# Layer 0's experts store rows in slot order by the sync queue, and GpSimd gathers each token's rows by slot in the middle phase

## The chip, the cores and the metric

The kernel runs on one core of a Trainium2 chip. The metric is the device time of one execution in microseconds (us). Names of engines: PE is TensorE, DVE is VectorE, ACT is ScalarE, POOL is GpSimd, SP is the sync engine, which computes nothing and issues DMAs. A DMA issued by GpSimd with a list of row numbers is called an indirect DMA here: a gather reads rows from DRAM by number, a scatter writes them by number.

## What is computed

Two transformer layers on x of shape 16 x 256 x 128 (4096 tokens of 128 numbers, f32). Each layer is an attention and a mixture of eight experts, both behind a layer norm, a modulation and a gate. For the change, this is what matters of layer 0's experts and what follows:

```python
logits = xt @ gate_w                                  # 4096 x 8
top_logits, top_idx = jax.lax.top_k(logits, 2)        # two experts for each token
router_probs = jax.nn.softmax(masked, axis=-1)        # over the two
exp_mask = exp_mask * (exp_rank < cap)                # a place beyond the capacity counts for nothing
h = gelu(einsum('ecd,edh->ech', exp_batches, c_fc) + fc_bias)      # d 128, h 512
exp_out = einsum('ech,ehd->ecd', h, c_proj) + proj_bias
out = einsum('nec,ecd->nd', cb_weight, exp_out)       # two weighted rows for each token
...
x = x + gb * out
h = layernorm(x) * (1 + ca) + sa                      # layer 1 starts: q, k, v and an importance
importance = (relu(h @ wi1.T + bi1) @ wi2.T + bi2)    # top 30% of keys by importance are kept
```

## The kernel before, in words

x stays in SBUF as 32 blocks (NT) of 128 tokens. Work on all tokens goes in NCH = 8 chunks of four blocks.

**Route phase.** Every (token, choice) pair is given a slot. Slots are ordered by expert in halves of 128; there are SC = 71 halves, in XTILES = 40 tiles: 31 pair tiles with two halves and 9 single tiles with one. DVE computes for each pair its slot (`slot_i`), and through one-hot matmuls the inverse: for each slot the token that it holds (`r.token`) and the row of `y_dram` to which its result goes (`r.dest`). `y_dram` has a row for each (choice, token) pair in token order, and further rows for the results of empty slots.

**Expert phase** (`expert_phase`, used by both layers; `gated` is true for layer 1 alone). For tile j GpSimd gathers the tokens' rows of `h_dram` (L2186), eight tiles ahead (ROWS). PE transposes them (L2023), ACT copies the transposed rows (L2083). PE multiplies with the first weights into `ps_h` (L2014), ACT applies gelu (L2075), PE multiplies with the second weights into `ps_o` (L2033), DVE adds the bias into `y` (L2121, `finish`). There are four buffers of `y` (UNROLL), and `y_free` waits until the store of the tile four before has landed. GpSimd scatters `y` into `y_dram` (L2196), one indirect DMA for each half. The weights of all experts lie in SBUF; since the expert of a tile is known only on the chip, ACT copies those of a tile into one of four working sets (`copy_weights`, L2052 to L2054), a tile ahead of use. SP loads weights of the next phase (`ahead`) and the `gates`, waits until all stores have landed, and issues `choice_rows` for the first two chunks (LEAD): for each chunk and choice one plain load of 256 KB from `y_dram` into `got`. The block ends with a barrier of all engines.

**Middle phase** (`middle_phase`). SP issues `choice_rows` for chunks 2 to 7. For each chunk ACT scales the first choice's rows (`weigh`, L1164), DVE adds the scaled second choice's rows (L1249), GpSimd multiplies with the gate (`gate`, L1083), DVE adds to x (L1231) and takes mean and variance, ACT and DVE form `std`, `rstd` and `shift` (L1257), ACT normalizes (L1176), PE transposes, ACT modulates, PE and ACT form queries, keys, values and the importance, and DVE counts for each key how many are more important (`rank`, L1276). The engines' orders are written by hand over steps i = 0 to 10; ACT's step i begins with `weigh(i + 1)`, DVE's has `statistics(i - 1)`, `weigh(i)`, `invert(i - 1)`, `rank(i - 3)` and `keys_values(i - 2)`. Between the first two gates GpSimd fills three constant tables: `before`, `head_mask` and `places` (L1086 to L1097). Layer 1's sparse attention comes next.

Layer 1's experts run `expert_phase` with `gated` and end in a final phase with the same kinds of loads. They keep their order.

Of the kernel before, what the change touches and what calls it, by code (L numbers as in the profile page):

```python
# [18 lines left out]
P = 128  # L19
# [996 lines left out]

def middle_phase(nc, k, r, a):
# [6 lines left out]
    with ExitStack() as ctx:  # L1024
# [9 lines left out]
        before = sb("before", [P, 2, T])  # L1034
# [22 lines left out]
        back, h_ready, const_ready = sem("back_m"), sem("h_ready_m"), sem("const_ready_m")  # L1057
        w_turned, w_copied, wi2_ready, pool_step = sem("w_turned1"), sem("w_copied1"), sem("wi2_ready"), sem("pool_step_m")
# [10 lines left out]
        @block.sync  # L1069
        def _(sp):  # L1070
            for n in range(LEAD, NCH):
                choice_rows(sp, k, r, n)

        @block.gpsimd
        def _(pool):
            step = Chain(pool, pool_step)

            def gate(n):
                pool.wait_ge(both_ready, 4 * (n + 1))
                if n == 0:  # L1080
                    pool.wait_ge(gates_in, 16)
                y = view(both[:, n % 2, 0, :], 0, [[2 * C, 2], [C, 2], [1, C]])
                pool.tensor_tensor(y, y, view(gates[:, 2 * n, :], 0, [[C, 2], [0, 2], [1, C]]), ALU.mult).then_inc(gated, 1)  # L1083

            gate(0)
            step(pool.memset(before[:, :, :], -TINY))  # L1086
            step(pool.affine_select(out=before[:, :, :], in_=before[:, :, :], compare_op=ALU.is_gt, fill=0.0, base=0,
                                    pattern=[[P, 2], [-1, T]], channel_multiplier=1))

            step(pool.memset(a.head_mask[:, :], 1.0))  # L1090
            for p in range(4):
                m = a.head_mask[4 * HD * p:4 * HD * (p + 1), :]
                step(pool.affine_select(out=m, in_=m, compare_op=ALU.is_ge, fill=0.0, base=0,
                                        pattern=[[-HD, 4]], channel_multiplier=1))
                step(pool.affine_select(out=m, in_=m, compare_op=ALU.is_ge, fill=0.0, base=HD - 1,
                                        pattern=[[HD, 4]], channel_multiplier=-1))
            pool.iota(a.places[:, :], [[1, KEPT]], base=0, channel_multiplier=0,  # L1097
                      allow_small_or_imprecise_dtypes=True).then_inc(const_ready, 1)
            for n in range(1, NCH):
                gate(n)  # L1100
# [126 lines left out]
        def _(dve):  # L1227
            def statistics(n):
                dve.wait_ge(gated, n + 1)
                xs = k.x[:, 4 * n:4 * n + 4, :]  # L1230
# [20 lines left out]

            def invert(n):
# [13 lines left out]
            def rank(n):  # L1266
                dve.wait_ge(col_turned, n + 1)
                if n == 0:
                    dve.wait_ge(const_ready, 1)
# [13 lines left out]
            for i in range(STEPS):  # L1283
# [417 lines left out]
def route_phase(nc, k, r, name, biased, capacity, weights):  # L1701
# [7 lines left out]
    with ExitStack() as ctx:  # L1709
# [27 lines left out]
        slot_i, part_i = sb("slot_i", [P, KT], I32), sb("part_i", [P, 2, KT], I32)  # L1737
# [59 lines left out]
        def _(dve):  # L1797
# [100 lines left out]
            step(dve.tensor_scalar(r.token[:, :], token_f[:, :], 0.0, None, ALU.max))  # L1898
            step(dve.scalar_tensor_tensor(out=free[:, :], in0=owner[:, :], scalar=0.0, in1=slot_id[:, :],
# [11 lines left out]

def choice_rows(sp, k, r, n):
# [7 lines left out]
def expert_phase(nc, k, r, name, weights, gated, ahead):  # L1920
# [10 lines left out]
    with ExitStack() as ctx:  # L1931
# [41 lines left out]

        def moved(j, ring=UNROLL):
# [4 lines left out]
        def _(sp):  # L1979
# [66 lines left out]
        def _(act):  # L2046
# [10 lines left out]
            if resident:  # L2057
                act.wait_ge(r.weights_in, 16 * E * (nf + 1))
                act.wait_ge(tables_in, 16 * (nf * FK + nr))
                if gated:  # L2060
                    act.wait_ge(halved, 1)
                copy_weights(0)
                copy_weights(1)
            for n in range(-1, XTILES + 1):
# [15 lines left out]
                if exists(n):  # L2080
# [3 lines left out]
                    if resident and exists(n + 1) and n >= 1:  # L2084
# [3 lines left out]
        def _(dve):  # L2088
# [22 lines left out]
            def y_free(j):  # L2111

                wait(dve, stored[j % UNROLL], 16 * moved(j - UNROLL))
                dve.nop(nofuse=True)

            def finish(j):
# [5 lines left out]
                                  each(out_b, j), ALU.add).then_inc(y_ready, 1)  # L2122

# [35 lines left out]
            held = {}  # L2159
            for j in range(-1, XTILES + 1):  # L2160
# [11 lines left out]
                elif exists(j):  # L2172
                    finish(j)

        @block.gpsimd
        def _(pool):
# [24 lines left out]
            for j in range(XTILES + 1):  # L2201
                if not gated and exists(j - 1):
                    scatter(j - 1)
# [3 lines left out]
                if exists(j + ROWS):  # L2207
# [3 lines left out]
                    elif j == 0:  # L2211
# [3 lines left out]
                if gated and exists(j - 1):  # L2215
                    scatter(j - 1)

# [70 lines left out]
def experts(nc, d, k, name, layer, gate_w, gate_b, capacity, weights, gated, ahead, then):  # L2288
    with ExitStack() as ctx:
# [5 lines left out]
        r.token, r.dest = sb("token", [P, SC], I32), sb("dest", [P, SC], I32)  # L2295
# [160 lines left out]
```

## Time and profile before

| what | us |
|---|---|
| median of 3 runs | 1230.93 (1228.71 to 1234.88) |
| the profiled execution | 1231.63 |
| its span, first to last instruction | 1229.9 |
| layer 0's experts, first gather to last scatter landed | 505.6 to 688.8 |
| middle phase, first to last instruction | 692.3 to 768.1 |
| busy in the span: PE, DVE, ACT, POOL | 1005.9, 802.4, 780.4, 779.9 |

The mean granted clock of TensorE is 0.931 of full speed. The times of the sections below count from the span's start. "Busy" for GpSimd includes its indirect DMAs; DMA issues of SP are not counted as busy. A difference of two kernels' times is read against the profiled execution's own time where it is worked out from the trace, and against the median where runs are compared.

### The profile page before, as it was taken

To read this page: it belongs to the slowest core of one execution; us is meant where nothing else is said; L and a number is where in the kernel's file an instruction comes from. 1 tells how busy PE (TensorE), PEld (TensorE's weight loads), DVE (VectorE), ACT (ScalarE), POOL (GpSimd) and SP (SyncE) were. 2 spreads that over 40 slices of the span, in tenths; PEclk is the share of its full clock that TensorE was granted. 3 is DMA by queue.
4 is the path that set the end of the run, shared out by engine and by line. 5 is a ranking of instruction groups with operands and counts; after the bars stand their busy time and mean duration, and the time that the engine had idled before them with its cause. 6 is when DMAs were issued, how large, how long until landed. Compare 5 with 4: busy or idle time off the path is not lost. (4 is left out here: it accounts for less than half of the span.)

```text
span 1229.9 us, 40087 instructions
## 1 busy us (share of the span) xinstructions
PE 1005.9 (82%) x16123; PEld 804.0 (65%) x16123; DVE 802.4 (65%) x1636; ACT 780.4 (63%) x1706; POOL 779.9 (63%) x807
## 2 busy tenths in 40 slices
PE   6789999999999964698776387799976599999970
PEld 4467777777777763698666243565644579988870
DVE  6678888887887858410000277699977747676775
ACT  5355555555655633687556475577764689988983
POOL 6667687688677530477777410788860178888864
PEclk9789999999999987799999699799997789999995
DMA  4733232222321025211112500200009411111117
GB/s 131 157 71 55 51 58 54 54 53 53 60 52 26 8 54 171 77 53 51 51 53 52 158 1 1 73 7 6 6 4 241 122 46 45 44 47 47 42 34 211
DMA packets 120840, 79.32 MB, mean 64 GB/s; under 512 B 44144, under 2 KB 111120, under 8 KB 120528
## 3 DMA queue, kind: packets, MB, share of 16 engines
q1 hardware_dynamic: 111568, 58.12, 20.8%
q0 software_dynamic: 9088, 18.63, 5.1%
q8 instruction: 129, 2.11, 0.7%
q14 instruction: 55, 0.45, 0.1%
HBM read 58.15 MB, written 17.76 MB: 62 GB/s over the span
## 5 line engine op out<-in xcount | busy, mean ns | idle before, releaser
L2075 ACT ACTIVATE act_x_m<-ps_h_x_m,fc_bias_x_m 128x256 f32<-128x256 f32 (+1 forms) x480 | 185.2, 470 | 66.5 <-PE ps_h_x_m L2014 60.5
L2014 PE MATMUL ps_h_x_m<-x_T_x_m,fc_x_m 128*128 128x256 f32 (+1 forms) x960 | 205.2, 365 | 4.4 <-ACT x_T_x_m L2083 2.3
L967 ACT ACTIVATE probT<-ps_t 128x512 f32<-128x512 f32 (+1 forms) x208 | 118.6, 594 | 140.8 <-PE ps_t L795 139.6
L2186 POOL DMA_INDIRECT x_rows_x_m<-h_dram,token_m x142 | 140.2, 987 | 96.5 <-POOLq L1709 57.0
L2014 PEld LDWEIGHTS ps_h_x_m<-x_T_x_m,fc_x_m 128*128 128x128 f32 x960 | 166.7, 196 | 23.9 <-issue 6.3
L2196 POOL DMA_INDIRECT y_dram<-y_x_m,dest_m x142 | 142.0, 1000 | 48.0 <-issue 40.6
L2033 PE MATMUL ps_o_x_m<-proj_x_m,act_x_m 128*128 128x128 f32 x1136 | 144.5, 279 | 33.0 <-DVE y_x_m L2121 25.4
L2033 PEld LDWEIGHTS ps_o_x_m<-proj_x_m,act_x_m 128*128 128x128 f32 x1136 | 133.8, 193 | 42.2 <-ACT act_x_m L2075 26.7
L717 POOL TENSOR_TENSOR rel_y<-rel_raw,own_rows 128x1024 f32<-128x1024 f32 x64 | 130.6, 2045 | 22.6 <-ACT rel_raw L975 22.6
L897 DVE TENSOR_REDUCE neg_max<-ps_s 128x8 f32<-128x512 f32 (+1 forms) x64 | 95.4, 1491 | 67.8 <-PE ps_s L780 67.7
L2121 DVE TENSOR_TENSOR y_x_m<-ps_o_x_m,out_rows_m 128x256 f32<-128x256 f32 (+1 forms) x40 | 15.8, 394 | 164.2 <-DMA y_dram<-y_x_m,dest_m 120.9
L795 PE MATMUL ps_t<-ident,prob 128*128 128x128 f32 x640 | 96.5, 286 | 8.2 <-ACT prob L960 7.8
L900 DVE TENSOR_TENSOR prob<-ps_s,neg_max 128x512 f32<-128x512 f32 (+1 forms) x64 | 95.4, 1491 | 2.2
L960 ACT ACTIVATE prob<-prob 128x512 f32<-128x512 f32 (+1 forms) x64 | 81.4, 1272 | 22.9 <-DVE prob L900 22.9
L906 DVE TENSOR_REDUCE row_sum<-prob 128x8 f32<-128x512 f32 (+1 forms) x64 | 94.4, 1475 | 0.0
L795 PEld LDWEIGHTS ps_t<-ident,prob 128*128 128x128 f32 x640 | 69.5, 143 | 25.8 <-issue 11.1
L211 POOL TENSOR_TENSOR q_rel<-q_spread,t_mask 128x2048 f32<-128x2048 f32 x16 | 73.3, 4581 | 13.6 <-DMA q_spread<-q_dram 13.6
L731 POOL TENSOR_TENSOR inv_diag<-row_inv,own_query 128x1024 f32<-128x1024 f32 x16 | 30.6, 1913 | 75.0 <-DVE row_inv L910 75.0
L780 PE MATMUL ps_s<-e_rel,q_rel 64*32 64x136 f32 (+13 forms) x4096 | 74.1, 259 | 3.9 <-issue 3.9
L1543 ACT ACTIVATE probT<-ps_t 128x512 f32<-128x512 f32 (+1 forms) x96 | 53.7, 594 | 34.5 <-PE ps_t L1413 33.9
L2052 ACT ACTIVATE fc_x_m<-fc_all_m 128x512 f32 (+1 forms) x80 | 69.3, 866 | 8.1 <-issue 4.2
L768 PE MATMUL ps_s<-kT,q_diag 32*128 32x32 f32 (+7 forms) x1024 | 56.1, 332 | 14.6 <-DVE prob L900 10.7
(309 smaller groups left out, 2118.6 us busy)
## 6 DMA issues: line engine op xcount, KB each, us to landing
q_spread<-q_dram SPq DMA_DIRECT2D x256, 64.0 KB
got_m<-y_dram SPq DMA_DIRECT2D x32, 256.0 KB, 5.0
h_dram<-h_rows_m SPq DMA_DIRECT2D x16, 256.0 KB, 2.4
x_rows_x_m<-h_dram,token_m POOLq DMA_INDIRECT x142, 2.6
y_dram<-y_x_m,dest_m POOLq DMA_INDIRECT x142, 2.3
x<-L_attn_x SPq DMA_DIRECT2D x8, 256.0 KB, 3.8
q_dram<-qT SPq DMA_DIRECT2D x8, 256.0 KB, 12.0
gates<-gate_dram SPq DMA_DIRECT2D x16, 128.0 KB, 4.3
```

Of the source, the lines that this page charges most:

```text
L717: pool.tensor_tensor(view(rel_y[:, u % 3, 4 * (m % 2), 0, :], 0, [[16, 4 * H], [4, 4], [1, 4]]), view(rel_raw[:, m % 3, :], 0, [[4, 4 * H] ...
L795: x = pe.transpose(ps_t[:, t % 2, p * P:(p + 1) * P], prob[:, m % 2, p, u * P:(u + 1) * P], k.ident[:, :])
L897: dve.tensor_reduce(neg_max[:, m % 2, :, :], split(ps_s[:, 0, :], m), AX.X, ALU.max, negate=True).then_inc(maxed, 1)
L900: dve.tensor_tensor(split(prob[:, m % 2, 0, :], m), split(ps_s[:, 0, :], m), view(neg_max[:, m % 2, :, :], 0, [[2, GROUPS], [1, 2], [0, n] ...
L906: dve.tensor_reduce(row_sum[:, b % 2, :, 2 * j:2 * j + 2], split(prob[:, m % 2, 0, :], m), AX.X, ALU.add).then_inc(summed, 1)
L960: act.activation(p_, p_, ACT.Exp).then_inc(expd, 1)
L967: act.activation(probT[to:to + n, store(m, ch), :, (2 * j + s) % 4, :], ps_t[row:row + n, t % 2, :].rearrange("p (g c) -> p g c", g=GROUPS ...
L2014: m = pe.matmul(ps_h[:, l, g, f % 2, 0:w], fc[:, slot, l, f * P:(f + 1) * P], x_T[:, slot % 2, 0:w], start=True, stop=True)
L2033: m = pe.matmul(ps_o[:, s % 2, h * P:(h + 1) * P], act1[:, s % 2, f, h * P:(h + 1) * P], proj[:, s, f, :], start=f == 0, stop=f == FK - 1)
L2075: m = act.activation(out[:, slot % 2, f, 0:w], ps_h[:, l, g, f % 2, 0:w], ACT.Tanh if l else ACT.Gelu, scale=0.5 if l else 1.0, bias=fc_bi ...
L2186: pool.indirect_dma_start(out=x_rows[:, slot, h, :], out_offset=None, in_=k.h_dram, in_offset=bass.IndirectOffsetOnAxis(ap=r.token[:, c:c ...
L2196: pool.indirect_dma_start(out=k.y_dram, out_offset=bass.IndirectOffsetOnAxis(ap=r.dest[:, c:c + 1], axis=0), in_=y[:, slot, h, :], in_offs ...
```

## The change

In layer 0's experts the results are no longer scattered. SP stores the rows of a tile as they are, in slot order, into a new tensor `slot_dram` of 71 x 128 rows. The rows of a chunk are brought back by `slot_rows` on GpSimd: for each choice and block of 128 tokens one gather from `slot_dram` by the pair's slot, eight for a chunk and 64 in all. GpSimd issues those of the first two chunks at the end of the expert phase, when all stores have landed, and the others in the middle phase, where they take the place of SP's loads. The gate moves from GpSimd to DVE there, and the constant tables are filled by GpSimd in the expert phase, behind its gathers (`place_tables`). The weight copies of layer 0 move from ACT to DVE, three tiles ahead. GpSimd's gathers of tokens from tile 9 on wait for the transposes of the tile eight before. In the route phase two DVE steps that formed `r.dest` fall away for layer 0. SP loads `gates` after its stores. Layer 1 is as before.

```diff
+def slot_rows(pool, k, r, n):
+    for c in range(TOPK):
+        for t in range(4 * n, 4 * n + 4):
+            pool.indirect_dma_start(out=r.got[:, c, t, :], out_offset=None, in_=k.slot_dram,
+                                    in_offset=bass.IndirectOffsetOnAxis(ap=r.slot[:, c * NT + t:c * NT + t + 1], axis=0)
+                                    ).then_inc(r.rows_in[n], 16)
...
 middle_phase:
-        @block.sync
-        def _(sp):
-            for n in range(LEAD, NCH):
-                choice_rows(sp, k, r, n)
         @block.gpsimd
         def _(pool):
-            (gate(0), the constant tables, gate(1) ... gate(7))
+            for n in range(LEAD, NCH):
+                slot_rows(pool, k, r, n)
...
-                act.wait_ge(rows_in[n], 16 * TOPK)
+                act.wait_ge(rows_in[n], 16 * 4 * TOPK)
...
 DVE's step i:
                 if chunk(i - 1):
                     invert(i - 1)
+                if chunk(i):
+                    gate(i)
...
 route_phase:
             step(dve.tensor_scalar(r.token[:, :], token_f[:, :], 0.0, None, ALU.max))
+            if r.slot is not None:
+                return
...
 expert_phase, SP:
             if ahead:
                 ahead(sp)
+            for j in range(0 if gated else XTILES):
+                at, n = P * first_half(j), halves(j)
+                sp.wait_ge(y_ready, j + 1)
+                sp.dma_start(k.slot_dram[at:at + P * n, :].rearrange("(h p) c -> p h c", p=P),
+                             y[:, j % UNROLL, 0:n, :]).then_inc(stored[j % UNROLL], 16)
             sp.dma_start(r.gates[:, :, :], ...)
             for i in range(UNROLL):
-                sp.wait_ge(stored[i], 16 * moved(XTILES - 1 - (XTILES - 1 - i) % UNROLL))
-            for n in range(LEAD):
+                sp.wait_ge(stored[i], 16 * written(XTILES - 1 - (XTILES - 1 - i) % UNROLL))
+            for n in range(LEAD if gated else 0):
                 choice_rows(sp, k, r, n)
...
 expert_phase, ACT: copy_weights for gated alone
...
 expert_phase, DVE:
+            def copy_weights(n):
+                s = n % UNROLL
+                wait(dve, act_ready, 2 * nf * (n - UNROLL + 1))
+                e = dve.value_load(r.expert[0:1, n:n + 1], min_val=0, max_val=E - 1)
+                dve.tensor_copy(fc[:, s, :, :].rearrange("p l f -> p (l f)"), r.fc[:, bass.ds(e, 1), :, :].rearrange("p o l f -> p (o l f)"))
+                dve.tensor_copy(fc_bias[:, s, :], fc_biases[:, bass.ds(e, 1), :, :].rearrange("p o l f -> p (o l f)"))
+                dve.tensor_copy(proj[:, s, :, :].rearrange("p f c -> p (f c)"),
+                                r.proj[:, bass.ds(e, 1), :, :].rearrange("p o f c -> p (o f c)")).then_inc(w_copied, 1)
...
+            if not gated:
+                dve.wait_ge(r.weights_in, 16 * E * (nf + 1))
+                for j in range(3):
+                    copy_weights(j)
...
                 elif exists(j):
                     finish(j)
+                    if exists(j + 3):
+                        copy_weights(j + 3)
...
 expert_phase, GpSimd:
             for j in range(XTILES + 1):
-                if not gated and exists(j - 1):
-                    scatter(j - 1)
...
-                    elif j == 0:
+                    else:
                         pool.wait_ge(x_turned, j + 1)
                         pool.nop(nofuse=True)
                     gather(j + ROWS)
...
+            if not gated:
+                for i in range(ROWS):
+                    pool.wait_ge(x_in[i], 16 * moved(XTILES - 1 - (XTILES - 1 - i) % ROWS, ROWS))
+                pool.nop(nofuse=True)
+                aside(pool)
+                for i in range(UNROLL):
+                    pool.wait_ge(stored[i], 16 * written(XTILES - 1 - (XTILES - 1 - i) % UNROLL))
+                pool.nop(nofuse=True)
+                for n in range(LEAD):
+                    slot_rows(pool, k, r, n)
```

`aside(pool)` is `place_tables`, with the operations that stood in the middle phase.

## Rows read from the trace of the kernel before

**Rows 1.** Groups by line, 505 to 690 us: count, busy, mean ns, idle before.
```profile
L2052 ACT ACTIVATE fc_x_m<-fc_all_m 128x512 f32 x40 | 25.4, 635 | 4.5 <-issue 4.2
L2121 DVE TENSOR_TENSOR y_x_m<-ps_o_x_m,out_rows_m 128x256 f32<-128x256 f32 (+1 forms) x40 | 15.8, 394 | 164.2 <-DMA y_dram<-y_x_m,dest_m 120.9 <-PE ps_o_x_m L2033 43.3
```

**Rows 2.** Timeline, GpSimd alone: start us, us, [idle before <-releaser].
```profile
505.56 1.24 POOL L2186 DMA_INDIRECT x_rows_x_m<-h_dram,token_m  x1 [57.01 <-POOLq L1709]
507.10 0.95 POOL L2186 DMA_INDIRECT x_rows_x_m<-h_dram,token_m  x1 [0.30 <-issue]
...
686.47 0.97 POOL L2196 DMA_INDIRECT y_dram<-y_x_m,dest_m  x1 [0.30 <-issue]
...
1050.62 1.24 POOL L2186 DMA_INDIRECT x_rows_x_m<-h_dram,token_m  x1 [0.18 <-issue]
```

**Rows 3.** Timeline of all engines, pair tiles 2 and 3.
```profile
521.87 1.89 PE L2014 MATMUL ps_h_x_m<-x_T_x_m,fc_x_m 128*128 128x256 f32 x8
...
525.61 1.89 PE L2014 MATMUL ps_h_x_m<-x_T_x_m,fc_x_m 128*128 128x256 f32 x8
...
526.72 1.65 ACT L2075 ACTIVATE act_x_m<-ps_h_x_m,fc_bias_x_m 128x256 f32<-128x256 f32 x4 [0.68 <-PE ps_h_x_m L2014]
...
527.55 1.95 PE L2033 MATMUL ps_o_x_m<-proj_x_m,act_x_m 128*128 128x128 f32 x16
```

**Rows 4.** Timeline of all engines, two of the single tiles.
```profile
678.18 1.13 PE L2014 MATMUL ps_h_x_m<-x_T_x_m,fc_x_m 128*128 128x128 f32 x8
...
679.23 1.12 ACT L2075 ACTIVATE act_x_m<-ps_h_x_m,fc_bias_x_m 128x128 f32<-128x128 f32 x4
...
680.62 1.13 PE L2014 MATMUL ps_h_x_m<-x_T_x_m,fc_x_m 128*128 128x128 f32 x8
```

**Rows 5.** Timeline between the phases: SP's issues and ACT's first instruction.
```profile
688.78 0.93 SPq L1916 DMA_DIRECT2D got_m<-y_dram  x2
689.20 1.61 SPq L1916 DMA_DIRECT2D got_m<-y_dram  x3
...
692.34 1.28 ACT L1203 ACT_TABLE_LOAD   x1 [9.81 <-PEq L1931]
```

**Rows 6.** Timeline of all engines, middle phase.
```profile
698.13 0.52 POOL L1086 MEMSET before<- 128x512 f32 x1
...
701.50 0.16 DVE L1257 SCALAR_TENSOR_TENSOR shift<-moments_x,rstd 128x4 f32<-128x4 f32 x1
...
701.64 0.19 POOL L1097 IOTA places<- 128x76 f32 x1
...
737.21 1.24 ACT L1164 ACTIVATE ps_part<-got_m,weight_m 128x128 f32<-128x128 f32 x4
...
740.15 1.26 POOL L1083 TENSOR_TENSOR both<-both,gates_m 128x512 f32<-128x512 f32 x1 [6.30 <-DVE both L1249]
740.19 1.24 DVE L1257 SCALAR_TENSOR_TENSOR shift<-moments_x,rstd 128x4 f32<-128x4 f32 x1
...
767.57 0.08 DVE L1276 DVE_READ_ACCUMULATOR compared<-imp_row,imp_col,before 128x1 f32 x1
```

**Rows 7.** The page's DMA issues: count, KB each, median us to landing.
```profile
h_dram<-h_rows_m SPq DMA_DIRECT2D x16, 256.0 KB, 2.4
x_rows_x_m<-h_dram,token_m POOLq DMA_INDIRECT x142, 2.6
```

**Rows 8.** Groups by line, GpSimd, 990 to 1205 us (layer 1's experts).
```profile
L2186 POOL DMA_INDIRECT x_rows_x_m<-h_dram,token_m x63 | 63.5, 1008 | 15.4 <-issue 15.4
```

**Rows 9.** Groups by line and shape, DVE, whole span.
```profile
L1263 DVE TENSOR_TENSOR kv<-ps_kv,bkv 128x512 f32<-128x512 f32 x16 | 10.6, 685 | 7.4 <-PE ps_kv L1123 7.4
...
L1899 DVE SCALAR_TENSOR_TENSOR free_m<-owner_m,slot_id_m 128x71 f32<-128x71 f32 x2 | 0.5, 232 | 0.1
...
L147 DVE COPY ident_w_n_m<-ident 128x128 f32<-128x128 f32 x2 | 0.4, 212 | 0.0
```

**Rows 10.** Stretches of 2 us, PE: busy, granted clock, DMA share, GB/s.
```profile
746.00:748.00 2.00, 2.00 (x3) 0.50 0.00 0
```

More of the change, by code:

```diff
@@ L1014, with place_tables @@
 TINY = 2.0 ** -126
+def place_tables(pool, a, done):
+    step = Chain(pool, done)
+    before = a.before
+    step(pool.memset(before[:, :, :], -TINY))
+    step(pool.affine_select(out=before[:, :, :], in_=before[:, :, :], compare_op=ALU.is_gt, fill=0.0, base=0,
+                            pattern=[[P, 2], [-1, T]], channel_multiplier=1))
+    step(pool.memset(a.head_mask[:, :], 1.0))
+    for p in range(4):
+        m = a.head_mask[4 * HD * p:4 * HD * (p + 1), :]
+        step(pool.affine_select(out=m, in_=m, compare_op=ALU.is_ge, fill=0.0, base=0,
+                                pattern=[[-HD, 4]], channel_multiplier=1))
+        step(pool.affine_select(out=m, in_=m, compare_op=ALU.is_ge, fill=0.0, base=HD - 1,
+                                pattern=[[HD, 4]], channel_multiplier=-1))
+    step(pool.iota(a.places[:, :], [[1, KEPT]], base=0, channel_multiplier=0, allow_small_or_imprecise_dtypes=True))
 def middle_phase(nc, k, r, a):
@@ L1917, in choice_rows, with expert_phase @@
                      k.y_dram.rearrange("(n p) c -> p n c", p=P)[:, first:first + 4, :]).then_inc(r.rows_in[n], 16)
-def expert_phase(nc, k, r, name, weights, gated, ahead):
+def expert_phase(nc, k, r, name, weights, gated, ahead, aside):
     nf = len(weights.fc)
@@ L1972, in count, with written @@
             return j // UNROLL + 1
+        def written(j):
+            return moved(j) if gated else len(range(j, -1, -UNROLL))
         def moved(j, ring=UNROLL):
@@ L2111, in y_free @@
             def y_free(j):
-                wait(dve, stored[j % UNROLL], 16 * moved(j - UNROLL))
+                wait(dve, stored[j % UNROLL], 16 * written(j - UNROLL))
                 dve.nop(nofuse=True)
@@ L2285, in _, with experts @@
             sp.wait_ge(stored, 16 * NCH)
-def experts(nc, d, k, name, layer, gate_w, gate_b, capacity, weights, gated, ahead, then):
+def experts(nc, d, k, name, layer, gate_w, gate_b, capacity, weights, gated, ahead, aside, then):
     with ExitStack() as ctx:
@@ L2315, in experts, with layer0_experts @@
         r.rows_in = [phase_semaphore(nc, k, f"rows_in{n}_" + name) for n in range(NCH)]
-        expert_phase(nc, k, r, "_x" + name, weights, gated, ahead)
+        expert_phase(nc, k, r, "_x" + name, weights, gated, ahead, aside)
         then(r)
-def layer0_experts(nc, d, k, ahead, then):
+def layer0_experts(nc, d, k, ahead, aside, then):
     w = Place()
@@ L2324, in layer0_experts @@
     w.rows = [d["L0_ffn_proj_bias"]]
-    experts(nc, d, k, "_m0", 0, d["L0_ffn_gate_w"], None, CAPACITY, w, False, ahead, then)
+    experts(nc, d, k, "_m0", 0, d["L0_ffn_gate_w"], None, CAPACITY, w, False, ahead, aside, then)
 def layers_between(nc, d, k):
@@ L2350, in ahead, with aside @@
                 sparse_loads(sp, d, a)
+            a.before = tb("before", [P, 2, T])
+            pool_step = phase_semaphore(nc, k, "pool_step_m")
+            def aside(pool):
+                place_tables(pool, a, pool_step)
             def then(r):
                 middle_phase(nc, k, r, a)
-            layer0_experts(nc, d, k, ahead, then)
+            layer0_experts(nc, d, k, ahead, aside, then)
             clear_semaphores(nc, k)
@@ L2367, in then @@
         final_phase(nc, d, k, r)
-    experts(nc, d, k, "_m1", 1, d["L1_ffn_Wr"], d["L1_ffn_br"], None, w, True, None, then)
+    experts(nc, d, k, "_m1", 1, d["L1_ffn_Wr"], d["L1_ffn_br"], None, w, True, None, None, then)
 class Place:
```

52 lines of the change are left out of this document (18 added, 34 removed).

## The prediction, made before the change was timed

> **What bounds the kernel now.** I read first the groups by line of layer 0's experts (505 to 690 us). DVE's bias addition is 15.8 us of work behind 164.2 us of idle time, 120.9 of it until a scatter of `y` has landed; ACT spends 635 ns on each large weight copy, of which a tile has two [rows 1]. The timeline of GpSimd explains it: an indirect DMA takes 0.95 to 0.97 us and the next starts 0.30 us later (the idle time is put down to "issue": GpSimd waits for nobody), so each costs 1.25 to 1.28 us of GpSimd [rows 2]. Layer 0 issues 71 gathers and 71 scatters: 142 x 1.28 = 182 us, and from the first gather at 505.6 to the last scatter at 686.5 it is 181 us [rows 2]. So the experts of layer 0 are bound by GpSimd's issuing.
>
> What the experts would do without that is seen in their first tiles, where the four `y` buffers still let PE run ahead: `ps_h` starts at 521.87 and 525.61, 3.73 us (3.74 by these two) per pair tile, and the two layers' matmuls fill it: 1.89 + 1.95 = 3.84 us of PE, which overlap a little. ACT waits 0.68 us for PE in each tile, so ACT does not set this period [rows 3]. For a single tile (9 of 40) the distance is 2.44 us, with ACT's gelus 1.05 us behind PE's start because a weight copy was still running [rows 4].
>
> Between the phases stands a barrier: SP sees the last scatter landed at 688.78, issues four loads until 690.8, and every other engine starts the middle phase at 692.34, released by the end of the block (L1931) [rows 5]. In the middle phase GpSimd has one product of 1.26 us per chunk and otherwise waits; `weigh(7)` begins on ACT at 737.21 and the last work of the phase ends at 768.05 (one comparison of 0.48 us starts with the last but one read-out, at 767.57) [rows 6].
>
> **The change, part by part.**
>
> *Route phase.* Two DVE steps fall away, of 232 ns each (one is shown) and a short gap: 0.5 us earlier [rows 9].
>
> *Experts.* GpSimd keeps the 71 gathers: 2.5 us per pair tile against PE's 3.73, so they are hidden, and they now wait for `x_turned`, eight tiles ahead. SP's stores carry the same 128 KB a tile and are issued by an engine that is free; a store of SP lands in 2.4 us [rows 7], which four buffers cover. PE then sets the pace. `ps_h` of tile 2 is at 521.87; tile 31 is 29 x 3.73 = 108.2 later, 630.0, less the 0.5 above: 629.5. The step that still holds the last pair's second layer takes 3.1 us (1.1 + 0.1 + 1.9), then seven single tiles at 2.3 us (between PE's work, half of 3.84 and some gaps, 2.1, and today's 2.44; without ACT's copy the gelus start about as early as PE allows): 648.7 for tile 39. Behind it come the gelus, second layer, addition and issue (3.7 us in all) and the landing, 2.4: the last row is stored at 654.8. Before it was 688.8. Gain 34.0 us. Bounds: if a pair tile takes 3.63 us, 3 us more; 3 us less if the copies cost something.
>
> *Weight copies.* On DVE a copy of 128x128 f32 takes 212 ns and an addition of 128x512 685 ns [rows 9]. A 128x512 copy thus lies between 0.21 and 0.69; I take the middle, 0.45. With the small one (0.1) that is 1.0 us a tile (1.6 at the upper end), and with the addition of 0.42 DVE is busy 1.4 to 2.0 us of 3.73, and at most 1.9 of 2.3 in single tiles. `copy_weights(j + 3)` stands behind `finish(j)` and is needed more than a tile later. Cost nothing; taking 1.5 us a tile off ACT gains nothing either, since ACT already waited for PE.
>
> The Trainium skill (SBUF — State Buffer, section "SBUF: two separate sides") speaks against this part: a DVE copy of fp32 within SBUF takes the port pair that GpSimd needs to write descriptors, and whoever starts first blocks the other for its whole instruction. The nearest row agrees that there is such a lock: DVE's tiny `shift` takes 1.24 us when it starts beside GpSimd's product, and 0.16 when it starts alone [rows 6]. By this rule each of the 120 copies could wait for a gather or delay one; it is a rival below.
>
> *Tables.* `place_tables` (698.13 to 701.83, 3.7 us, in the middle phase before [rows 6]) now runs on GpSimd after its last gather, around 632, while PE still has 20 us of tiles. Uncovered it would cost 3.7.
>
> *The first two chunks.* GpSimd must see all stores landed, then issues 16 gathers before it reaches the barrier: 15 x 1.25 + 0.95 + 0.3, since the first of a run is longer (1.24) [rows 2], = 20.0 us with PE, ACT and DVE idle. Barrier 1.5 us as before. So the middle phase starts at 654.8 + 20.0 + 1.5 = 676.3; from the last landing to its start it is 21.5 us where it was 3.5: loss 18.0. SP's 1 MB `gates` load now sits behind its stores, but 20 us hide it.
>
> *Middle phase.* 48 gathers follow, 8 per chunk. Beside a busy DVE (layer 1) a gather takes 1.008 us [rows 8], so I take 1.30 us each: 10.4 us per chunk. They are queued behind nothing, as the product is gone from GpSimd. The rows of chunk 7 are there at 47 x 1.30 + 2.6 [rows 7] = 63.7 us after the start, where `weigh(7)` began at 44.9 before. ACT waits for them first in its step, and everything else of the phase has by then caught up. Behind `weigh(7)` lay 30.8 us before (737.21 to 768.05). It should be 1.5 us less: DVE's sums of that step are done ahead and `shift` no longer waits for GpSimd's product (1.24 against 0.16 [rows 6]), which pays for the product itself (0.69 a chunk, now on DVE). So 29.3. The phase is 63.7 + 29.3 = 93.0 where it was 75.7: loss 17.3. SP's 12 loads that disappear were ahead of need.
>
> **Sum.** -34.0 + 18.0 + 17.3 = +1.3 us. The profiled execution took 1231.63 us (span 1229.9 and 1.7 around it), so 1232.9; it lies 0.7 above the median of 1230.93, so against the median I expect 1232.
>
> **Rivals.**
>
> *A, slower: gathers of the middle phase are slower than 1.30.* There DVE is the busiest engine, mostly with operands from SBUF. For: single gathers of layer 1 take 1.24 [rows 2]. Against: their mean is 1.008. If all 48 took 1.24 + 0.30 = 1.54, this adds 47 x 0.24 = 11.3: 1243. It decides (over 0.5%, 6.2 us) from 0.1 us per gather on. The Trainium skill (SBUF — State Buffer, section "Who interferes with whom") says that a DVE instruction with two SBUF inputs blocks a GpSimd instruction that reads SBUF.
>
> *B, slower: PE's clock.* In the middle phase PE will work some 6.5 of 10.4 us per chunk. Before, at a greater share, the granted clock fell once to 0.50, in 746 to 748 [rows 10], where matmuls take twice as long. Some 1.5 us of a step's chain are matmuls that nothing hides, so a fall costs about 1.5 in its step. If it happens in three of the last steps (it counts only behind `weigh(7)`), +4.5: 1237.
>
> *C, slower: the copies wait for gathers in the experts, as `shift` waits for the product [rows 6].* The place is the start, where GpSimd issues 16 gathers without pause: nine copies that each wait for a gather would take 9 x 1.25 = 11.3 us instead of 3 [rows 2], and tile 3's weights come 1 to 3 us late. Later, gathers and copies together are 2.5 + 1.0 of 3.73 us and still fit. +2 to +4: 1235.
>
> *D, faster: the experts are held by more than the weight loads.* If ACT's copies are in the 3.73 us loop after all, a pair tile takes 3.5 and a single 2.1: 29 x 0.23 + 7 x 0.2 = 8 us: 1224. Against: ACT's wait of 0.68.
>
> *E: the change doesn't do what it says,* the experts stay bound by issuing. For this the gathers alone would have to fill 3.73 us; at 2.5 they don't. Price: the 34 us of the experts back, 1266.
>
> **How the numbers follow.** Chances: the sum as it stands 0.48, A 0.17, B 0.12, C 0.06, D 0.15, E 0.02. The time is the sum's, 1232. Within 0.5% (1224.8 to 1237.1, about what a measurement of this kernel can tell from no change) lie the sum, C and half of B, less its own tails: 0.51. Slower: A, half of B, E and a tail, 0.30. Faster: D and a tail, 0.19. The range goes from D's 1224 to 1244, which takes in A; the sum's own range is 1227 to 1238 (3 us either way in the experts, 1.25 to 1.35 per gather, 27 to 32 us behind `weigh(7)`).
>
> **What would show it.** Last store landed near 655 and PE at 3.73 us per pair tile; 16 gathers with all other engines idle, 20 us; the middle phase starting near 676 and ending near 769; in it ACT waiting for `got`, and GpSimd never idle until some 60 us in. DVE's 128x512 copies near 0.45 us. The prediction is wrong if the gathers in the middle phase are spaced by more than 1.4 us, if the barrier doesn't hold the other engines, or if the experts end before 650 or after 660.

## The result, and the profile after

| | median us | runs | profiled execution | span | mean clock |
|---|---|---|---|---|---|
| before | 1232.82 (1228.71 to 1235.27) | 8 | 1231.63 | 1229.9 | 0.931 |
| changed | 1237.76 (1236.01 to 1240.07) | 8 | 1239.61 | 1237.5 | 0.915 |

The ratio is 1.0039, with a 95% interval of 1.0022 to 1.0056. That is within 0.5%, the case that the prediction gave 0.51, but the interval does not reach down to 1: in this comparison the changed kernel is 4.9 us slower by the medians, where +1.3 was forecast. The 1237.76 lies 5.8 us above the 1232, inside the range, and 0.7 above the 1237.1 at which the prediction set its upper 0.5%: the kernel before came out 1.9 us higher in this comparison (1232.82) than when the prediction was made (1230.93).

The two profiled executions differ by 7.6 us of span, and not all of it is the change's. Layer 0's first gather stands at 508.28 where it stood at 505.56 [rows 2], 2.7 us later. In the eleven traces other than that of the kernel before (the changed kernel twice, and the experiments), this time lies anywhere from 503.6 to 512.1, without relation to their edits (the whole of the attention stands before it). Behind the middle phase the rest of the program took 462.3 us before and 461.3 to 466.2 in the eleven others. So all readings here are made by stretch, from the first gather to the last read-out of `rank(7)`:

| stretch, us | before | forecast | changed |
|---|---|---|---|
| first gather to last row stored | 183.2 | 149.7 | 146.8 |
| last row stored to start of the middle phase | 3.6 | 21.5 | 27.1 |
| start of the middle phase to `weigh(7)` | 44.9 | 63.7 | 64.4 |
| `weigh(7)` to the last read-out | 30.4 | 29.3 | 27.4 |
| sum | 262.0 | 264.2 | 265.7 |

The stretch grew by 3.7 us. (The forecast's +1.3 also took in 0.5 for the route phase, and began from 262.5: it took the read-out at 767.57 for the last but one, where it is the last, and so set before's end 0.4 us too late.)

Groups by line of the changed kernel's experts, 504 to 680 us (busy us, mean ns, idle time before):

```profile
L2031 PE MATMUL ps_h_x_m<-x_T_x_m,fc_x_m 128*128 128x256 f32 (+1 forms) x320 | 70.6, 364 | 2.3 <-ACT x_T_x_m L2099 2.0
...
L2217 POOL DMA_INDIRECT x_rows_x_m<-h_dram,token_m x71 | 68.1, 959 | 111.5 <-POOLq L1705 56.7 <-PE ps_x_x_m L2040 37.4 <-issue 14.7
...
L2144 DVE COPY fc_x_m<-fc_all_m 128x512 f32 x40 | 17.2, 431 | 16.0 <-issue 15.9
...
L2137 DVE TENSOR_TENSOR y_x_m<-ps_o_x_m,out_rows_m 128x256 f32<-128x256 f32 (+1 forms) x40 | 15.8, 395 | 80.3 <-PE ps_o_x_m L2050 80.3
```

These rows answer to [rows 1]. DVE's bias addition does the same 15.8 us of work, but its 120.9 us of waiting for landed scatters are gone: it waits for PE. GpSimd waits 37.4 us for PE's transposes, so it is no longer what the experts are bound by. PE has 2.3 us of idle time in front of 70.6 us of first-layer matmuls: PE is. The copies take 431 ns on DVE.

Timeline of the experts' end, of PE and SP (start us, us):

```profile
623.71 1.89 PE L2031 MATMUL ps_h_x_m<-x_T_x_m,fc_x_m 128*128 128x256 f32 x8
...
627.45 1.89 PE L2031 MATMUL ps_h_x_m<-x_T_x_m,fc_x_m 128*128 128x256 f32 x8
...
646.87 1.13 PE L2031 MATMUL ps_h_x_m<-x_T_x_m,fc_x_m 128*128 128x128 f32 x8
...
649.05 1.13 PE L2031 MATMUL ps_h_x_m<-x_T_x_m,fc_x_m 128*128 128x128 f32 x8
...
653.08 0.43 SPq L2012 DMA_DIRECT2D gates_m<-gate_dram  x1
```

A pair tile takes 3.74 us, as at the start of the kernel before [rows 3]; a single one takes 2.18, where [rows 4] had 2.44.

Timeline of the border of the two phases and of the middle phase, GpSimd, ACT and DVE:

```profile
508.28 1.32 POOL L2217 DMA_INDIRECT x_rows_x_m<-h_dram,token_m  x1 [56.72 <-POOLq L1705]
...
655.08 0.97 POOL L1915 DMA_INDIRECT got_m<-slot_dram,slot_m  x1 [16.77 <-DMA slot_dram<-y_x_m]
...
673.83 0.94 POOL L1915 DMA_INDIRECT got_m<-slot_dram,slot_m  x1 [0.30 <-issue]
...
682.20 1.28 ACT L1192 ACT_TABLE_LOAD   x1 [31.23 <-PEq L1939]
...
682.84 0.94 POOL L1915 DMA_INDIRECT got_m<-slot_dram,slot_m  x1 [8.07 <-SPq L1041]
...
744.05 0.94 POOL L1915 DMA_INDIRECT got_m<-slot_dram,slot_m  x1 [0.30 <-issue]
...
746.58 1.24 ACT L1153 ACTIVATE ps_part<-got_m,weight_m 128x128 f32<-128x128 f32 x4 [3.69 <-DMA got_m<-slot_dram,slot_m]
...
773.95 0.08 DVE L1270 DVE_READ_ACCUMULATOR compared<-imp_row,imp_col,before 128x1 f32 x1
```

The 16 gathers run from 655.08 to 674.77, 19.7 us (forecast 20.0). Then something stands here that the forecast did not have: GpSimd is done at 674.77, and ACT starts the middle phase at 682.20, 7.4 us later. Before, the start came 1.5 us behind the end of SP's last issue [rows 5], and the forecast took SP for the last to come to the barrier. In the middle phase the remaining 48 gathers start 1.30 us apart on the average (682.84 to 744.05, 47 steps), and ACT waits for their rows before each of the last six `weigh`.

The waits of the changed kernel between 500 and 790 us, summed (who waits <- for what: us in total, times, longest):

```profile
POOL x_rows_x_m L2217 <- PE ps_x_x_m L2040: 37.4, 21, 2.8
...
ACT L1192 <- PEq L1939: 31.2, 1, 31.2
...
ACT ps_part L1153 <- DMA got_m<-slot_dram,slot_m: 29.1, 6, 7.6
```

In the experts GpSimd waits for PE, in the border ACT waits 31.2 us for the barrier, and in the middle phase it waits 29.1 us for gathered rows: the experts' old bound, GpSimd's issuing, is now the middle phase's.

### The profile page after: what moved, and what is told of

Read it like the earlier page. It is cut to its first block and busy times, and to the rows that moved or that the text cites. A ratio compares the mean times of both kernels' runs of the same rounds, so it can differ in the third digit from the quotient of the medians.

```text
span 1237.5 us, 40065 instructions
## 1 busy us (share of the span) xinstructions
PE 1003.0 (81%) x16123; PEld 804.3 (65%) x16123; DVE 835.5 (68%) x1762; ACT 734.0 (59%) x1586; POOL 762.1 (62%) x792
## 5 line engine op out<-in xcount | busy, mean ns | idle before, releaser
L2050 PE MATMUL ps_o_x_m<-proj_x_m,act_x_m 128*128 128x128 f32 x1136 | 142.0, 277 | 6.2 <-DVE act_x_m L2115 5.5
L717 POOL TENSOR_TENSOR rel_y<-rel_raw,own_rows 128x1024 f32<-128x1024 f32 x64 | 130.5, 2040 | 24.1 <-ACT rel_raw L975 24.1
L1915 POOL DMA_INDIRECT got_m<-slot_dram,slot_m x64 | 62.9, 983 | 43.7 <-issue 18.9
L2227 POOL DMA_INDIRECT y_dram<-y_x_m,dest_m x71 | 72.4, 1020 | 26.4 <-issue 19.3
L2137 DVE TENSOR_TENSOR y_x_m<-ps_o_x_m,out_rows_m 128x256 f32<-128x256 f32 (+1 forms) x40 | 15.8, 395 | 80.3 <-PE ps_o_x_m L2050 80.3
```

The source lines that it names most:

```text
L717: pool.tensor_tensor(view(rel_y[:, u % 3, 4 * (m % 2), 0, :], 0, [[16, 4 * H], [4, 4], [1, 4]]), view(rel_raw[:, m % 3, :], 0, [[4, 4 * H] ...
L2050: m = pe.matmul(ps_o[:, s % 2, h * P:(h + 1) * P], act1[:, s % 2, f, h * P:(h + 1) * P], proj[:, s, f, :], start=f == 0, stop=f == FK - 1)
```

## The experiments

Two theories stood first. **Gathers**: what the change costs is the 64 gathers, wherever they stand; 16 in front of the middle phase or in it are the same. **Barrier**: GpSimd coming last to the barrier has a price of its own, apart from what it does there. Each kernel ran on the same chip as the kernel before, beside it; three of them ran once, the others 4 to 12 times. "The stretch" is always that from the first gather to the last read-out.

**The changed kernel again**

> The changed kernel again, as the mate of the others on this chip. Expected 1237.8 us, 5 above the kernel before, within 0.3%. In the first profile its middle phase began 27.2 us after the last store had landed: 19.8 to the end of GpSimd's 16 gathers (674.8) and 7.4 more to the first work of the other engines (682.2). The second should show the same two numbers.

Measured: 1236.0 us over 12 runs against 1235.32 of before, ratio 1.001 (0.9988 to 1.0032). Start of the middle phase 175.9 us behind the first gather (173.9 in the first trace), then 64.3 and 27.4 (64.4 and 27.4). So the anatomy repeats within 2 us, and the 7.4 us from GpSimd's last gather to the start stand there again, while the total is now no different from before's. Both together put the change at 0 to +0.5%.

The 2 us are tile 1's first layer on PE. The eight matmuls, and the granted clock where they ran:

| trace | tile 1's `ps_h`, us, and clock | first gather to tile 2 |
|---|---|---|
| before (from 516.26) | 3.75, at half | 16.3 |
| changed (from 519.08) | 1.96, at full | 14.6 |
| changed again (from 515.43) | 3.75, at half | 16.6 |

```profile
516.26 3.75 PE L2014 MATMUL ps_h_x_m<-x_T_x_m,fc_x_m 128*128 128x256 f32 x8 [1.19 <-ACT x_T_x_m L2083]
...
519.08 1.96 PE L2031 MATMUL ps_h_x_m<-x_T_x_m,fc_x_m 128*128 128x256 f32 x8 [1.40 <-ACT x_T_x_m L2099]
```

The first line is of the kernel before, the second of the changed one. Of the ten traces with the changed experts seven have the short time and three the long one, and the two traces of the changed kernel differ in it. So it is chance and not the change. By the second trace the stretch is 267.5 us, 5.5 above before's, with tile 1 at the same clock in both.

**All 64 gathers in the middle phase**

```diff
 middle_phase, GpSimd:
-            for n in range(LEAD, NCH):
+            for n in range(0, NCH):
                 slot_rows(pool, k, r, n)
 expert_phase, GpSimd, behind aside(pool):
-                for i in range(UNROLL):
-                    pool.wait_ge(stored[i], 16 * written(...))
-                pool.nop(nofuse=True)
-                for n in range(LEAD):
-                    slot_rows(pool, k, r, n)
```

> The 16 gathers of chunks 0 and 1 are moved behind the barrier; all 64 are issued in the middle phase. Theory: GpSimd's indirect DMAs ahead of the barrier cost their own 20 us of idle engines and lengthen the barrier from some 2 us to 7.4. Then the middle phase starts 3 us after the last store lands (before: 3.5), all 64 gathers in a row bring chunk 7 at 80.6 us after its start, and the whole is 4 to 5 us shorter than the changed kernel: 1233. Rival: the barrier is as long (7.4) whatever GpSimd did; then the start comes 7 us after the last landing and nothing is gained.

Timeline of this kernel, SP, ACT and GpSimd:

```profile
634.01 0.20 POOL L1031 IOTA places<- 128x76 f32 x1
...
648.98 0.43 SPq L2012 DMA_DIRECT2D gates_m<-gate_dram  x1
...
650.61 1.28 ACT L1192 ACT_TABLE_LOAD   x1 [3.75 <-PEq L1939]
...
651.24 0.96 POOL L1915 DMA_INDIRECT got_m<-slot_dram,slot_m  x1 [17.03 <-SPq L1041]
```

GpSimd is done at 634.2 and waits at the barrier. SP is last; the middle phase starts 1.6 us behind SP's issue of `gates`, which includes the landing of the last store. `weigh(7)` comes 84.7 us after the start (80.6 was expected) instead of 64.4: the 16 gathers are all paid here (20.3 us), as both theories say. What is gone is the 7.4 us. The stretch is 258.4 us, against 265.7 and 267.5 for the two traces of the changed kernel. The median, 1232.55 (0.9973 of before, 0.995 to 0.9996), is 3.5 us below the changed kernel's beside it, less than the 7 to 9 us of the traces. The 12 times fall in two groups, five from 1227.5 to 1228.9 and seven from 1231.8 to 1235.1; the profiled one is of the lower. What sets the upper group was not seen in a trace; tile 1's clock would make 2 of the 5 us between the groups.

**What makes the barrier dear: arithmetic, one gather, or a bare wait**

Three kernels are the one above with a single thing put back in front of GpSimd's barrier. `tables last` waits for the stores and then fills the tables; `one before` waits and issues one gather; `wait only` waits and does nothing.

```diff
 tables last:                        one before:                          wait only:
+    wait for stored[0..3]; nop           aside(pool)                          aside(pool)
     aside(pool)                     +    wait for stored[0..3]; nop      +    wait for stored[0..3]; nop
                                     +    slot_rows(pool, k, r, 0, 0, 1)
```

> As e1_all_in_middle, but GpSimd waits until all stores have landed and then fills the constant tables (3.7 to 4.2 us of its own arithmetic, no DMA) ahead of the barrier. If it is indirect DMAs that lengthen the barrier, the middle phase starts 1 to 3 us after the last table operation; if any late work of GpSimd lengthens it, 7.4 us after.

> As e1_all_in_middle, but one of the 64 gathers stays ahead of the barrier, behind the wait for all stores. If the delay of the barrier is one price for GpSimd coming late, the other engines start 6 to 7.5 us after that gather ends. If it grows with the DMAs that GpSimd has in flight (16 in the changed kernel), it is nearer to 3.

> As e1_all_in_middle (tables early, no gather ahead of the barrier), but GpSimd waits for all stores before it goes to the barrier, and does nothing behind that wait. The middle phase began 1.6 us after SP's last issue where GpSimd had come to the barrier long before (e1_all_in_middle), but 6.3 to 7.4 us after GpSimd's last instruction where it came last (the changed kernel, e2_tables_last). Theory: GpSimd needs some 5 to 6 us from its last wait to the barrier, whatever it did. Then the middle phase starts 5 to 6 us after the last store has landed, 5 later than in e1_all_in_middle. Rival: only work of GpSimd (arithmetic or DMA) makes the barrier late; then it starts within 2 us.

Timelines of GpSimd's last work (where there is any) and of ACT's first instruction, of `tables last` (with SP's issue of `gates`):

```profile
650.64 0.43 SPq L2012 DMA_DIRECT2D gates_m<-gate_dram  x1
652.01 0.52 POOL L1021 MEMSET before<- 128x512 f32 x1 [23.27 <-DMA slot_dram<-y_x_m]
...
655.47 0.19 POOL L1031 IOTA places<- 128x76 f32 x1
...
661.96 1.28 ACT L1192 ACT_TABLE_LOAD   x1 [13.44 <-PEq L1939]
```

of `one before`:

```profile
657.76 0.97 POOL L1914 DMA_INDIRECT got_m<-slot_dram,slot_m  x1 [16.68 <-DMA slot_dram<-y_x_m]
...
665.27 1.28 ACT L1192 ACT_TABLE_LOAD   x1 [11.64 <-PEq L1938]
```

and of `wait only`, SP and ACT:

```profile
651.38 0.43 SPq L2012 DMA_DIRECT2D gates_m<-gate_dram  x1
...
658.81 1.28 ACT L1192 ACT_TABLE_LOAD   x1 [9.56 <-PEq L1939]
```

| kernel | GpSimd's last thing in front of the barrier | us to the start of the middle phase |
|---|---|---|
| changed | 16 gathers | 7.4 (674.77 to 682.20) |
| one before | one gather | 6.5 (658.73 to 665.27) |
| tables last | arithmetic, no DMA | 6.3 (655.66 to 661.96) |
| wait only | a wait | 5.4 to 6.0 |
| before | scatters, with SP's four loads behind them | 4.9 (687.44 to 692.34) |
| all in middle | nothing in the last 16 us | none seen: SP's wait ends it |

For `wait only` the landing is not in the trace as an instruction; in the others GpSimd's first instruction behind it came 1.4 to 2.0 us behind SP's issue of `gates`, which puts it at 652.8 to 653.4 here. The comparison with `all in middle` needs no such estimate: behind the same issue of `gates` the middle phase starts 1.6 us later there and 7.4 us later here (651.38 to 658.81), and GpSimd's wait is the only difference. So the price is there without a DMA of GpSimd and without work: it is that of GpSimd arriving last, 5 to 6.5 us, and some 1 us more behind 16 gathers. Whether the kernel before paid it as well is not shown. Its 4.9 us from GpSimd's last scatter are also 1.3 to its landing and 3.6 with SP's four loads, so either engine can have come last; with SP's last issue ending at 690.8 the forecast read the barrier as 1.5.

The total times of these three are single ones (1237.05, 1243.5 and 1242.09), and their first gathers stand at 505.9, 510.7 and 506.6; by stretch they took 268.0, 265.5 and 267.2 us against 258.4 with nothing there. `wait only` has a second cost, behind `weigh(7)`: 30.7 us instead of 27.4. Its windows of 4 us there (PE, PEld, DVE, ACT and POOL busy, then PE's granted clock, DMA share and GB/s):

```profile
744.00:748.00 4.00, 3.01 (x4) 1.33 (x5) 2.67 (x13) 3.81 (x10) 0.00 (x0) 0.55 0.00 0
748.00:752.00 4.00, 3.40 (x13) 2.01 (x11) 3.31 (x14) 1.02 (x2) 0.00 (x0) 0.50 0.00 0
```

The clock was granted at half, 1.2 GHz instead of 2.4, right after `weigh(7)` (743.09). In the traces with 27.4 us it was full from 2 to 12 us behind `weigh(7)`. This is rival B's mechanism, at 3.3 us.

**The weight copies**

Rival C says that DVE's copies and GpSimd's descriptors hold each other up, rival D that ACT's copies had been in the experts' loop. One kernel is the kernel before with nothing but the copies on DVE (`copies alone`), where GpSimd is the bound. The other is `all in middle` with the copies back on ACT (`copies on ACT`), where PE is.

```diff
 copies alone, on the kernel before, DVE:
+            copy_weights(0), (1), (2) ahead of the first tile; ACT's for gated alone
                     finish(j)
+                    if exists(j + 3):
+                        copy_weights(j + 3)
 copies on ACT, on "all in middle": DVE's three places removed
-            if gated:
+            if resident:
                 (ACT's copy_weights, a tile ahead, as in the kernel before)
```

> The kernel before with the weight copies of layer 0 on DVE and nothing else changed. GpSimd's issuing is the bound there, so any time that a DVE copy takes from an indirect DMA is seen at once. In the changed kernel one gather in six grew from 0.94 to 1.04 to 1.19 us while GpSimd was issuing without pause. If that holds here, the stretch from the first gather to the last scatter (181.9 us) grows by 0.1 to 0.25 us a tile, 4 to 10 us: ratio 1.003 to 1.008. Rival: the copies cost nothing (the wait is taken in the idle 0.30 us between two DMAs): 1.000.

> e1_all_in_middle with the weight copies of layer 0 back on ACT, as in the kernel before, one tile ahead. Theory: in the changed experts PE's matmuls set the pace and ACT waited for PE already, so pair tiles stay at 3.73 us and the copies' place is worth nothing in them; the nine single tiles, whose gelus stand behind a copy on ACT, go from 2.2 to 2.4 us. The stretch from the first gather to the middle phase's start (146.4 in e1_all_in_middle) becomes 147 to 149. Rival: with ACT's 1.3 us of copies the pair tiles take longer than 3.73, and the stretch 155 or more.

Groups by line, first the scatters of the kernel before, then `copies alone`, 500 to 700 us:

```profile
L2196 POOL DMA_INDIRECT y_dram<-y_x_m,dest_m x71 | 69.9, 985 | 21.6 <-issue 21.0 <-DVE y_x_m L2121 0.6
...
L2210 POOL DMA_INDIRECT y_dram<-y_x_m,dest_m x71 | 74.9, 1055 | 22.6 <-issue 20.3 <-DVE y_x_m L2120 2.3
...
L2200 POOL DMA_INDIRECT x_rows_x_m<-h_dram,token_m x71 | 69.4, 977 | 78.3 <-POOLq L1709 57.0 <-issue 20.1 <-DVE y_x_m L2120 1.2
...
L2127 DVE COPY fc_x_m<-fc_all_m 128x512 f32 x40 | 20.9, 523 | 15.5 <-issue 13.8 <-ACT act_x_m L2074 1.5
```

A scatter takes 1055 ns instead of 985 in the kernel before, and a copy 523 ns instead of the 431 of the changed kernel: each holds the other up. The 70 ns on 71 scatters are 5.0 us, and GpSimd's first gather to its last scatter took 187.3 us against 180.9 [rows 2], +6.4. Another 1.0 is idle time of GpSimd: it waited 3.5 us for DVE's `y`, which now stands behind copies in DVE's order, where it was 0.6 before. The ratio is 1.0083 (1.0054 to 1.0112), at the upper end of what was expected; by the medians it is 8.9 us. The trace shows 6.4 in the experts and 4.7 over the whole stretch, so part of the 8.9 is not explained. The rule of the Trainium skill (SBUF — State Buffer, section "SBUF: two separate sides") that the prediction weighed agrees with this in its direction: a DVE copy of fp32 locks GpSimd out of the ports with which it writes descriptors.

Of `copies on ACT`, the last single tiles on PE:

```profile
645.61 1.13 PE L2031 MATMUL ps_h_x_m<-x_T_x_m,fc_x_m 128*128 128x128 f32 x8 [0.20 <-issue]
...
647.94 1.13 PE L2031 MATMUL ps_h_x_m<-x_T_x_m,fc_x_m 128*128 128x128 f32 x8 [0.20 <-issue]
```

Its pair tiles are again 3.73 us apart and its single ones 2.33 (2.18 with DVE's copies); from the first gather to the middle phase it took 147.3 us, 0.9 more than `all in middle` (tile 1 at full clock in both). The median is 1234.37, ratio 0.9993 (0.9976 to 1.001). So where PE is the bound, moving the copies to DVE gained 1 us, in the single tiles, and nothing in the pair tiles: rival D is refuted. And where GpSimd has time to spare, the lock costs nothing that these traces show: rival C is real in its mechanism and hidden here. At the start of the changed experts, where rival C had its price, the nine copies of the first three tiles took 2.9 us beside GpSimd's gathers (508.64 to 511.55), and not 11.3.

**The gate on GpSimd, between the gathers**

```diff
 middle_phase, GpSimd:
+            def gate(n): (as in the kernel before)
+            gate(0)
             for n in range(LEAD, NCH):
                 slot_rows(pool, k, r, n)
+                gate(n - 1)
+            gate(NCH - 1)
 DVE's step: gate(i) removed
```

> The changed kernel with the gate of the middle phase back on GpSimd, between its gathers (gate(n - 1) behind the gathers of chunk n). GpSimd sets the pace there, so each product that stands ahead of the last gather costs its time, 1.26 + 0.1, six of them: 8 us more than the changed kernel, 1244 to 1246, and ratio 1.007 to 1.01 to the kernel before. Rival: DVE sets the pace too; then taking 0.69 us a chunk off it gives part back, and it comes within 4 us of the changed kernel.

Timeline of GpSimd at the start of the middle phase (which ACT began at 681.63):

```profile
686.23 1.26 POOL L1093 TENSOR_TENSOR both<-both,gates_m 128x512 f32<-128x512 f32 x1 [12.03 <-DVE both L1248]
687.64 1.43 POOL L1923 DMA_INDIRECT got_m<-slot_dram,slot_m  x1
```

The time is 1248.23 us, ratio 1.014 (1.0094 to 1.0185); the expectation was too low. `gate(0)` waits for DVE's sums, and all gathers wait behind it: the first starts 6.0 us into the phase instead of 0.6, which costs 5.4 us that the expectation had left out. The chain from the first to the last gather has five products in it (the expectation counted six) and grew from 61.2 to 66.0 us, 4.8; and `weigh(7)` comes 74.4 us after the start instead of 64.4. GpSimd's chain of gathers is the bound of the phase: what it grew by came out at `weigh(7)`. The products lengthen five gaps between gathers from 0.30 to 1.45 to 1.57 us, 6.0 in all; 1.1 came back because the gathers got shorter, from 996 to 972 ns on the mean, with the gate gone from DVE.

**ACT's `weigh` at the end of its step**

In the changed kernel ACT's step i begins with `weigh(i + 1)`, which waits for gathered rows, and behind this wait stand the normalization and all other work of chunks whose rows have long come.

```diff
 on "all in middle", ACT's step i:
-                if chunk(i + 1):
-                    weigh(i + 1)
                 (std, normalize, modulate of the earlier chunks)
+                if chunk(i + 1):
+                    weigh(i + 1)
```

> As e1_all_in_middle, and ACT's weigh(i + 1) is moved from the front of its step i to the end. Theory: in the changed middle phase GpSimd sets the pace, ACT waits 4 to 5 us for rows at the front of each step and holds back work on older chunks that could run; when the last rows arrive, one step more than needed is left. Moved, the stretch behind the last weigh falls from 27.4 us by a step's 6 to 7, so 1226 to 1228. Rival: other waits of the step (DVE's order, PE's) take its place and it stays within 2 us of e1_all_in_middle.

> e4_weigh_last once more, as the mate of e8_copies_act on this chip: 1226, ratio 0.990 to 0.995, so that the gain of both edits together is seen in a second call.

Timeline of this kernel, ACT and DVE:

```profile
735.37 1.24 ACT L1153 ACTIVATE ps_part<-got_m,weight_m 128x128 f32<-128x128 f32 x4 [3.89 <-DMA got_m<-slot_dram,slot_m]
...
759.45 0.08 DVE L1270 DVE_READ_ACCUMULATOR compared<-imp_row,imp_col,before 128x1 f32 x1
```

It ran in two comparisons, on two chips. Behind `weigh(7)` there are 24.1 us instead of 27.4 (24.0 in the second trace), half of the 6 to 7 that were expected. With the shorter time in front (83.3 against 84.7) the two parts of the middle phase gained 4.7 us on `all in middle`. The stretch is 255.9 us in both traces, the shortest of all, though tile 1 ran at half clock in both. The median is 1226.12, ratio 0.9926 (0.9899 to 0.9954), and on another chip 1223.31, ratio 0.9898 (0.9877 to 0.992). The direction was right, the size was not; the clock is one reason that can be seen. Window of this kernel, columns as above:

```profile
740.00:750.00 10.00, 9.40 (x26) 4.75 (x25) 6.51 (x27) 4.96 (x11) 0.00 (x0) 0.64 0.01 2
```

PE is busy 9.4 of 10 us right behind `weigh(7)`, at a clock of 0.64. In both traces of this kernel the clock stood at 0.50 from 2 to 10 us behind `weigh(7)`, as in `wait only`, where it came with 3.3 us more. That is the size of the missing 3 us; no run of this kernel at full clock there shows it. This is the version that beats both kernels.

## Why the prediction came out as it did

*What bounds the kernel before* was right: with the scatters gone from GpSimd the experts run at PE's period, 3.74 us forecast as 3.73.

*The experts* came out 2.9 us shorter than forecast. Tile 2 stands 14.6 us behind the first gather where the forecast had 16.3, since tile 1's first layer happened to run at full clock: 1.7 us, and luck, for in the second trace of the changed kernel it is 16.6. The single tiles, from the first to the last, took 18.0 instead of 19.2 (most of them 2.18 instead of 2.3 apart): 1.2 us, a term that was a little high. The copies at 0.431 and 0.424 us were forecast as 0.45. Rival E (the change doesn't do what it says) is out.

*The first two chunks* hold the term that was mis-sized. The prediction wrote "Barrier 1.5 us as before". The 1.5 was the distance from SP's last issue to the start, and it was carried over to a barrier at which GpSimd comes last. With GpSimd last it is 7.4 us; before, it was 4.9 from GpSimd's last scatter, a distance that could have been read from the same rows and warned of this. This term was 5.9 too low, the gathers' 0.3 too high. `all in middle`, `wait only`, `tables last` and `one before` show that it hangs on GpSimd's arrival and not on the gathers.

*The middle phase* was forecast as 93.0 and took 91.8. The gathers' spacing of 1.30 us was right, taken from layer 1's mean [rows 8]; most are 1.25 apart, and in most chunks one or two take longer. The four longest (1.31 to 1.47) start within 0.2 us of DVE's gate:

```profile
706.72 0.69 DVE L1246 TENSOR_TENSOR both<-both,gates_m 128x512 f32<-128x512 f32 x1
706.75 1.47 POOL L1915 DMA_INDIRECT got_m<-slot_dram,slot_m  x1 [0.30 <-issue]
...
717.27 1.31 POOL L1915 DMA_INDIRECT got_m<-slot_dram,slot_m  x1 [0.30 <-issue]
```

Seven of the 48 gathers took more than 1.05 us here, and two of 48 with the gate on GpSimd. So rival A's mechanism is there, but with 1.54 for each it did not come. Behind `weigh(7)` 27.4 us stand for the forecast 29.3. The wrong end accounts for 0.4 of this; that the other engines caught up further than assumed while ACT waited for rows is the likely rest, and was not tested.

*Rival B*, the clock: it fell in the middle phase, where the gathers set the pace and the fall is hidden, and was full again behind `weigh(7)`. Two windows of the changed kernel:

```profile
730.00:740.00 10.00, 8.14 (x21) 3.69 (x20) 6.10 (x24) 5.05 (x14) 7.82 (x8) 0.67 0.19 50
...
750.00:760.00 10.00, 8.12 (x35) 4.13 (x34) 9.60 (x38) 7.13 (x15) 0.00 (x0) 1.00 0.01 2
```

In `wait only` it fell behind `weigh(7)`, and there it cost 3.3 us. So the condition that the prediction set, that it counts only there, is borne out by these traces.

*The sum*: −2.9 in the experts, +5.6 in front of the middle phase, −1.2 in it make +1.5 beside the forecast, which is the difference of 265.7 and 264.2. The change itself is thus worth +3.7 us by one trace, +5.5 by the other, and 0 to +0.5% by the two comparisons. The mechanism was right, the loss behind the experts taking back their gain; the size of one term was not. Part of it was offset: by 1.7 us of luck in tile 1, and by small terms that were too high. In the second trace, without this luck, the stretch came 3.3 us above the forecast. The direction is not settled: +1.3 was forecast, and of the two intervals one lies above 1 and one includes it. In the profiled execution another 3.2 us of the difference to the forecast is the first gather's later start, which is no part of the change.

What stays open: what GpSimd does in the 5 to 7 us after its last instruction; what decides tile 1's clock; why `all in middle` has two groups of times; and how the first gather's time comes to vary by 8 us between kernels that are almost the same up to there.

## What to carry to other kernels

Read the price of a barrier from each engine's last instruction to the others' first one, not only from the engine that seems to come last in one trace; and if GpSimd has nothing left that the others need, let it come to the barrier first. Work that binds an engine on one side of a barrier (142 indirect DMAs in the experts) is not gained when it is moved to where that engine becomes the bound again (64 gathers of 1.25 to 1.30 us each, 16 in front of the middle phase and 48 in it): 36.4 us were gained in the experts and 40.1 given back behind them. When transfers set the pace, an in-order engine should wait for them at the end of its step, behind the work that is already possible; that order alone was worth 6.4 us here by the medians (1232.55 to 1226.12 on the same chip) and 4.7 in the traces of the middle phase.

## What the runs showed of the hardware

- With GpSimd last at the barrier, 5.4 to 7.4 us passed from its last instruction or wait to the others' first instruction: 7.4 behind 16 gathers, 6.5 behind one, 6.3 behind arithmetic, 5.4 to 6.0 behind a bare wait. Where GpSimd had been done for 16 us (`all in middle`), the others started 1.6 us behind SP's issue of `gates`, the landing of the last store included.
- The eight matmuls of a pair tile's first layer took 3.75 us at a granted clock of 0.50 and 1.89 to 1.97 at full clock; the same tile 1 of the same kernel had either in two traces.
- GpSimd issues an indirect DMA of 128 rows in 0.94 to 1.00 us and needs 0.30 between two, gather or scatter; beside DVE's fp32 copies scatters took 1.06 instead of 0.99 on the mean, and the copies of the first weights 0.52 instead of 0.43. The four gathers of the changed kernel that started within 0.2 us of DVE's gate took 1.31 to 1.47.
- A DVE copy of 128x512 f32 took 0.424 to 0.431 us, ACT's 0.635 to 0.648.
